# Attention over the edges of a graph: one sign change for the four row maxima of a step in place of one for each pair of heads

## The reference, cut to what matters

```python
scores = jnp.einsum('ehd,ehd->eh', q[origin], k[destination]) * SCALE
ws = scores * edge_weights
seg_max = jax.ops.segment_max(ws, origin, num_segments=N)
e = jnp.exp(ws - seg_max[origin])
denom = jax.ops.segment_sum(e, origin, num_segments=N)
att = e / (denom[origin] + 1e-16)
values = jax.ops.segment_sum(att[:, :, None] * v[destination], origin, num_segments=N)
```

## Time and profile before

| | before |
|---|---|
| median of 3 runs | 1080.33 us (1077.6 to 1081.13) |
| profiled execution, its time | 1079.38 us |
| profiled execution, its span | 1077.5 us |
| PE busy | 737.6 us (68%) |
| DVE busy | 544.0 us (50%) |
| ACT busy | 397.4 us (37%) |
| mean granted TensorE clock | 0.813 |

### The profile page before, as it was taken

How to read it: one execution, slowest core, us unless ns; L and a number is a source line. 1 busy time by engine, 2 the same in 40 slices (tenths; PEclk the granted TensorE clock), 3 DMA queues, 4 the chain that set the end, 5 groups by cost and what they waited for, 6 DMA issues and landing times.

```text
span 1077.5 us, 13741 instructions
## 1 busy us (share of the span) xinstructions
PE 737.6 (68%) x4498; PEld 436.4 (41%) x4537; DVE 544.0 (50%) x1269; ACT 397.4 (37%) x943; POOL 392.7 (36%) x401
## 2 busy tenths in 40 slices
PE   7744510494332211115999999999999999999996
PEld 4321100241001011003544454576766667767773
DVE  4601400482000110200532473888889999999998
ACT  2300001020000000001313020689989998877773
POOL 2677577477777776562572000000000000000002
PEclk9956655696555555556999999999999999999998
DMA  9788866536500000002400021444444444443323
GB/s 323 270 292 302 281 239 212 179 112 219 193 23 3 23 3 22 22 3 79 153 2 1 1 79 78 149 185 172 158 157 157 161 164 167 150 140 137 137 69 96
DMA packets 71115, 143.12 MB, mean 133 GB/s; under 512 B 22565, under 2 KB 57137, under 8 KB 67079
## 3 DMA queue, kind: packets, MB, share of 16 engines
q1 hardware_dynamic: 48884, 120.06, 30.7%
q10 hardware_dynamic: 8464, 15.84, 4.2%
q0 software_dynamic: 13696, 6.33, 3.1%
HBM read 77.47 MB, written 64.80 MB: 132 GB/s over the span
## 4 chain that ended last, share of the span: by engine, by line
PE 50%; another core or an unknown queue 20%; issue 20%; DVE 6%; ACT 2%; DMA 2%; ACTq 1%; DVEq 0%; POOLq 0%
PE bank L1092 11%; PE bank L1319 9%; PE bank L1364 7%; PE bank L1342 7%; PE bank L1077 6%; PE bank L1388 3%; PE bank L1326 2%; DVE AR L1841 1%; PE bank L1370 1%; DMA AR<-in_L_mix_bp_dram 1%; DVE QMN L1451 1%; DVE QMN L1450 1%; PE bank L1112 1%; DMA AR<-kv_rows,xd 1%
## 5 line engine op out<-in xcount | busy, mean ns | idle before, releaser
L630 POOL DMA_INDIRECT w_tab<-pay,idx x330 | 326.5, 989 | 160.0 <-issue 116.1
L1077 PE MATMUL bank<-AR 128*128 128x512 f32 (+1 forms) x288 | 130.9, 587 | 122.7 <-issue 102.8
L705 POOL DMA_INDIRECT AR<-kv_rows,xd x10 | 10.5, 1051 | 445.4 <-PE bank L1364 331.6
L1092 PE MATMUL bank<-AR 128*128 128x512 f32 (+1 forms) x240 | 128.6, 666 | 62.4 <-issue 62.4
L1077 PEld LDWEIGHTS bank<-AR 128*128 128x128 f32 x288 | 62.3, 222 | 180.3 <-issue 156.3
L1541 DVE TENSOR_TENSOR V<-bank,bias_row 128x512 f32<-128x512 f32 (+1 forms) x10 | 6.9, 691 | 250.0 <-remote 153.5
L912 ACT ACTIVATE AR<-AR,nmx 128x512 f32<-128x512 f32 (+1 forms) x180 | 118.5, 662 | 20.6 <-DVE nmx L1855 20.5
L1841 DVE CUSTOM_DVE_ANT_0 AR<-bank,AR,MX 128x512 f32<-128x512 f32 (+1 forms) x120 | 114.9, 986 | 8.6 <-remote 7.6
L1319 PE MATMUL bank<-KT,QT 64*128 64x512 f32 (+1 forms) x480 | 108.6, 568 | 4.0 <-ACT bank L920 3.7
L1092 PEld LDWEIGHTS bank<-AR 128*128 128x128 f32 (+1 forms) x240 | 48.3, 205 | 133.5 <-issue 133.0
L1364 PE MATMUL bank<-AR,V 128*64 128x128 f32 (+1 forms) x1520 | 101.9, 274 | 0.2 <-ACT AR L927 0.2
(11 more groups left out here) (272 smaller groups left out, 1013.2 us busy)
## 6 DMA issues: line engine op xcount, KB each, us to landing
w_tab<-ztile SPq DMA_DIRECT2D x20, 2280.0 KB
AR<-w_tab SPq DMA_DIRECT2D x20, 2048.0 KB, 7.4
AR<-w_tab SPq DMA_DIRECT2D x10, 1344.0 KB, 6.2
w_tab<-ztile SPq DMA_DIRECT2D x3, 1800.0 KB
w_tab<-pay,idx POOLq DMA_INDIRECT x330
w_tab<-ztile SPq DMA_DIRECT2D x2, 1700.0 KB
kv_rows<-AR ACTq DMA_DIRECT2D x9, 256.0 KB
kv_rows<-V ACTq DMA_DIRECT2D x9, 256.0 KB
```

Source lines behind the costliest of these rows:

```text
L630: pool.indirect_dma_start(out=w_tab, out_offset=bass.IndirectOffsetOnAxis(ap=idx[:, k, j:j + 1], axis=0), in_=pay[:, k % RING, j, :], in_o ...
L1077: last = mm(b[:, 0:n], w[:, k, m * P:(m + 1) * P], src_t(k), start=(k == 0), stop=(k == KC - 1))
L1092: last = mm(b[0:r, :], src_t(k)[:, 0:r], w[:, k, :], start=(k == 0), stop=(k == KC - 1))
```

## The change

The two sign changes of a step become one instruction over four maxima. It waits until all four `weighted` of the step have ended, stands right behind the fourth of them in every step, and counts `s_nm` up by two.

```diff
-            def shift_of(u):
-                w, p = u // 4, u % 4
+            def shifts_of(d):
+                w, q = d // 2, d % 2
                 g, c = w // NT, w % NT
-                for hh in range(2):
+                for u, hh in four(d):
                     gone(dve, ("s", u, hh))
-                v.tensor_scalar(nmx[:, u % 4, :], MX[g][:, c, 2 * p:2 * p + 2], -1.0, None, ALU.mult).then_inc(s_nm, 1)
+                v.tensor_scalar(nmx[:, 2 * q:2 * q + 2, :], MX[g][:, c, 4 * q:4 * q + 4].rearrange("p (u h) -> p u h", u=2), -1.0, None, ALU.mult).then_inc(s_nm, 2)
...
                     weighted(2 * d + 1, 0)
-                    if not late:
-                        shift_of(2 * d)
                     weighted(2 * d + 1, 1)
+                    shifts_of(d)
                     if d >= 1 and not late:
                         odd_of(2 * d - 1)
-                    if late:
-                        shift_of(2 * d)
-                    shift_of(2 * d + 1)
...
                     weighted(2 * d + 1, 0)
-                    shift_of(2 * d)
                     weighted(2 * d + 1, 1)
+                    shifts_of(d)
                     if w + 1 < NW:
                         mask(w + 1)
...
                     if 2 * NT <= w - 2:
-                        if d < ND - 1:
-                            added(w - 2)
-                        else:
-                            shift_of(2 * d + 1)
-                            added(w - 2)
-                    if d < ND - 1:
-                        shift_of(2 * d + 1)
+                        added(w - 2)
                     odd_of(2 * d - 2)
```

## The result

The changed kernel takes **1099.24 us**, the median of four runs (1092.70 to 1100.94), against 1080.73 for the kernel before with these runs (four, 1077.60 to 1083.22): a ratio of 1.0162, 95% interval 1.0111 to 1.0212 (ratios here and below are those on record, which leave out a few far slower executions of the kernel before; the quotient of two medians can differ a little from them, and is 1.0171 here). It is slower, by about as much as was forecast. The profiled execution took 1098.2 us, 18.8 more than that of before, so the two traces can be compared term by term.

What follows compares the result with a forecast made beforehand. PE was taken to bound the kernel, with ACT's mask arriving just in time. Group 0's 9.6 and group 1's 9.4 us sum to 19.0, added to the profiled 1079.38 for 1098.4, plus 0.95 to the median: 1099 us, range 1089 to 1104.

Steps and rivals of the forecast that it cites:

- The page names nobody: Groups 0 and 1: the profile page names nothing that waits for ACT, so starts were compared, giving 0.11 to 0.12 us.
- it costs nothing today: PE's wait for ACT's mask before the change: scores take 1.96 us with the late mask, 1.99 in the odd step.
- Group 0, 1.20 forecast: Odd step of group 0: exponentials, mask and PE's second load 1.20 us later in 8 tiles, 9.6 us.
- both exponentials (1.54 until the mask): ACT, odd step of group 0: queued behind the wait for the sign change, taking 1.54 us until the mask.
- Group 1, 1.04 forecast: Odd step 0.92 us later plus 0.12 from the even step, 1.04 a tile in 9 tiles, 9.4 us.
- 0.12 longer: DVE, even step of group 1: pays 0.26 us instead of 0.14, with no idle time ahead of the odd step.
- Several tenths: Sign in the profile: ACT waits for `nmx` in group 1's odd steps by several tenths of a us.
- Moved at no cost: Odd steps' second sign change, even steps of groups 0 and 1, and all of group 2: shifts that cost nothing.
- Half: Rival: in group 1 PE waits for `rescaled`, so only group 0 pays, 9.6 us, 1089.9; chance 0.12.
- More: Rival: delay goes round ACT and opens a second wait, 0.4 a tile for 17 tiles, 6.8 us, 1106; chance 0.07.
- Nothing: Rival: PE's second load doesn't wait for the mask; at most group 1 pays 1.1 us, 1080 to 1081.5; chance 0.08.
- Faster: Rival: DVE sets group 1's pace, each sign change less saves 163 ns in 20 steps, 3.3 us, 1077; chance 0.05.

Runs made afterwards that it cites:

- Even steps alone: One merged sign change behind the fourth multiplication in even steps only, odd steps as before, against the kernel before: 1076.60 us, ratio 1.0018.
- Group 2 alone: One merged sign change in place of two in group 2 only, groups 0 and 1 as before, against the kernel before: 1075.76 us, ratio 1.0001.
- before earlier: Kernel before, with the odd steps' first sign change one multiplication earlier, right behind the second, against the kernel before: 1079.77 us, ratio 1.0040.
- two behind the fourth: Two sign changes, each waiting for its own pair, both right behind the fourth multiplication, against the kernel before: 1090.57 us, ratio 1.0142.

## Why the prediction was right

**The path, right.** Exponentials late, mask late, PE's second load late: the loss is gone when that one mask is, and it comes without any change on DVE when the mask alone is moved. The load stands 0.11 behind the end of the mask, as forecast, in both groups. Two sentences of the reading were too strong. "The page names nobody" holds for the loads alone, as the page's row of PE's multiplications names ACT's masks, though before the change nearly all of its 3.7 us belong to other masks. And "it costs nothing today" held for 16 of the 17 tiles; in tile 11 this mask already cost 0.20. Tiles of 13.50 and 14.14 us, with 13.5 and 14.0 forecast; group 2 unchanged.

**The sum, right to 0.1 us, its terms not quite.** Forecast 9.6 and 9.4, found 8 times 1.08 or 8.6 and 9 times 1.14 or 10.3 (18.9 for 19.0). So two errors cancelled, and that is luck. Another two did so as well: the 0.8 us in tile 10 and at the passage to group 2, which the sum doesn't have, stand against the 0.8 by which the work ahead of tile 0 was shorter, so that the profiled execution came to 1098.2 with 1098.4 forecast.

- *Group 0, 1.20 forecast and 1.08 found.* The start of the exponentials was right: measured from PE's odd scores they are 1.24 later (728.03 to 732.56 before, 730.45 to 736.22 after). The term that failed is "both exponentials (1.54 until the mask)". Now the mask starts 1.42 behind the first exponential (736.22 to 737.64), and it lasts 0.58 and not 0.60. The other 0.12 before were a wait for DVE's `mask`, which ended at 734.06; that wait is gone now, as `mask` ends (736.71) well ahead of ACT's exponentials. 1.24 less 0.12 less 0.02 is 1.10, and the load is 1.09 later against the odd scores (6.79 and 7.88). I had read a distance between two starts on one engine as work, where a part of it was a wait that the view did not name.
- *Group 1, 1.04 forecast and 1.14 found.* The even step: "0.12 longer" was 0.19. The first odd multiplication starts 1.31 behind PE's odd scores before (866.94 to 868.24) and 1.50 after (866.56 to 868.06). The sign change starts 0.21 (even step, 866.74 to 866.95) to 0.23 (odd step) behind the readout, not the 0.19 that I took; the bounds of 0.12 to 0.30 held. Timelines of DVE, ACT and PE's loads, changed kernel, group 1:

```profile
872.36 0.09 DVE L1841 DVE_READ_ACCUMULATOR2_ANT MX<- 128x1 f32 x1
872.59 0.17 DVE L1855 TENSOR_SCALAR nmx<-MX 128x4 f32<-128x4 f32 x1
...
872.80 0.72 ACT L912 ACTIVATE bias_row<-bias_row,nmx 128x512 f32<-128x512 f32 x1 [1.02 <-DVE nmx L1855]
...
874.91 0.33 PEld L1319 LDWEIGHTS bank<-KT,QT 64*128 64x128 f32 x4 [1.70 <-issue]
```

Here the chain of starts is the same as in group 0: readout 872.36, sign change 872.59, exponentials 872.80, mask 874.22 to 874.80, load 874.91. "Several tenths" of waiting on ACT was too low; it is 1.0 us a step.

**Moved at no cost, right.** Even steps alone: 1.0018, not told from 1 (on top of the changed odd steps they cost the 0.20 a tile of group 1 that the sum has as 0.12). Group 2 alone: 1.0001.

**The rivals.** *Half* fell: group 1 pays as group 0 does, and without the mask it pays 0.13 a tile. The profile's attribution of PE's wait to `rescaled` was to a neighbour: in the kernel before `rescaled` ended at 860.88 and the load started at 861.16, 0.28 later, and 0.11 behind the mask. *More* didn't come: from 690 us on, all waits of PE but those for ACT's masks add up to 7.6 us, 7.7 before. That longer tiles left ACT its room was my reason, and isn't shown. *Nothing* fell with the kernel whose mask alone was moved. *Faster* fell: DVE won nothing in busy time or in place. The rule on which it leaned, that of the Trainium skill, page VectorE: DVE Perf Modes, section Rules for kernel authors, to minimize the count of operations and not the semaphores, doesn't agree with this trace: 60 operations of 163 ns fewer left DVE's busy time at 543.9 us (544.0 before). That the kernel is 1.6% slower is no evidence against the rule, as it comes from the place of the wait. The row of the rule also says not to fuse operations for speed, and with that the trace agrees: where the merge moved no mask, in group 2, it gained nothing (1.0001).

## What to carry to other kernels

Before merging small instructions, look at what each of them releases and at what stands in the queue behind the engine that waits: here the first sign change let ACT's exponentials start a microsecond earlier, and the mask queued behind them was what PE waited for. Here the mask had two predecessors on two engines that ended together, and a delay of either came back nearly one for one; moving one of them earlier should gain nothing while the other stays, but no run here moved one alone. When the profile puts an idle time down to "issue" or to a neighbour, find the releaser by the distance from its end to the start of what waits (0.11 to 0.12 us here, in every kernel in which ACT lays this mask), and look at the rows of the work behind the load: here the multiplications named the mask.

## What the runs showed that I had not expected

**The small instruction cost by its wait, not by its length.** A sign change right behind the readout that it waits for starts 0.18 to 0.19 behind the readout's start with two waits (before earlier; two behind the fourth: 0.35 for both, 0.16 for one) and 0.21 to 0.23 with four waits and four columns, which no run tells apart. One that needs nothing recent starts together with the readout and holds DVE for 0.06 to 0.10.
In group 2 the readout of a fourth now starts at 997.68 and the merged sign change at 997.89, for 0.17. So it ends 0.38 behind the readout's start, and the two together had ended 0.36 behind it: for whoever waits for the sign, the merge brought nothing even where both stood behind the fourth already.
